# Registers used as loaded, and a 32-deep ring of message tiles, in a graph network kernel

## The chip, the cores and the metric

The kernel runs on one core of a Trainium2 chip. The metric is the device time in microseconds of one execution; a measurement is a median over executions. The core has five engines that matter here: TensorE (PE, with its weight loads shown as PEld), VectorE (DVE), ScalarE (ACT), GpSimd (POOL) and SyncE (SP). Each runs its own instruction stream in order. A name with a q (DVEq, ACTq, SPq) is that engine's sequencer: register work, loads of registers and the issuing of DMAs.

## What is computed

The reference is two graph layers over 12,500 nodes of 128 features and 212,500 edges, each followed by a residual sum and a layer norm.

```python
# layer 0: message passing, summed at the source node of each edge
h = silu(edge_attr @ W1 + b1); weights = h @ W2 + b2
messages = node_feats[dst] * weights
aggregated = segment_sum(messages, src, N)
x = layernorm(x + concat([x @ Wself + bself, aggregated]) @ Wcat + bcat)
# layer 1: means of neighbours in both directions, then a GRU cell
a_in, a_out = seg_mean(feat_in[src], dst, N), seg_mean(feat_out[dst], src, N)
x = layernorm(x + gru_cell(concat([a_in, a_out]), x))
```

## The kernel before

The kernel goes through stages in order of time. It prepares weights and tables (0 to 650 us); it computes the edge messages and scatters them, sorted by source, into the DRAM tensor `msgs` (to 2516 us); it sums them by node, the first aggregation (to 3252 us); it updates the nodes (to 3506 us); it gathers and sums neighbour rows for both directions, the second aggregation (to 8020 us); and it runs the GRU.

**The first aggregation.** The sorted edges are cut into units of 256 edges, each of which falls in one block of 128 nodes. There are V0 = 928 units, in 29 iterations (IT0) of NS = 32. Where a unit begins (row 0 of `vtab` in DRAM) and where its block stands in the accumulator (`blk0` in SBUF) are data, so they are read into registers, 32 at a time, once per iteration. For each unit:

- SP (even units, line 431) or ACT (odd units, line 707) issues one DMA that loads 256 rows of `msgs` into a slot of `mtile`; they do so in `row_loads`, which begins each iteration with `load_table`: one load of 32 registers and one copy (`snap`) for each of them (lines 320 and 321). Each load waits in `need(..., s["sum0_ready"], it * NS + k - S0 + 1)` until TensorE has summed the unit that held the slot before.
- GpSimd (`keys0`, line 581) turns the node numbers of four units (a quad) into numbers within the block, `local`, once the quad has landed.
- VectorE (`onehot0`, line 1120) makes a one-hot matrix of each unit in `oh0`. It does this one quad ahead of its sums.
- TensorE (`sums0`, line 1498) multiplies one-hot and messages, two products of 128 x 128 x 128, into one of eight PSUM banks.
- VectorE (line 1138) adds the bank to the block's place in `acc_a`.

VectorE's stream in `sums0` is: load 32 registers from `blk0` (line 1124), copy them (line 1125), and then 32 times one one-hot of the next quad and one addition of this one. `mtile` and `oh0` both have S0 = 16 slots.

**The second aggregation** runs 55 iterations (IT1) of 32 units of 128 edges for each of two directions. SP loads 32 registers and issues 32 small DMAs of edge data into `edge2` (line 470); GpSimd issues 32 indirect gathers of node rows (line 605); VectorE makes one-hots (line 1245); TensorE sums (line 1542); VectorE adds (line 1256), at offsets from its own 32 registers, again read by `load_table`.

Of the kernel before, what the change touches and what calls it, by code (L numbers as in the profile page):

```python
# [4 lines left out]

N, E, D, A = 12500, 212500, 128, 8
P = 128
# [4 lines left out]
EP = NG * GE  # L13
T = NG * TG
NB = -(-N // P)
# [7 lines left out]
U0, U1 = 2 * P, P  # L23
NS = 32
V0 = -(-(E // U0 + NB) // NS) * NS
V1 = -(-(E // U1 + NB) // NS) * NS
CW = D + 1
# [48 lines left out]
def gnn_kernel(nc, x, src, dst, edge_attr, W1, b1, W2, b2, Wself, bself, Wcat, bcat,  # L76
# [15 lines left out]
    vtab = dram("vtab", [6, V1], i32)  # L92

    ctx = ExitStack()
    with ctx:
# [16 lines left out]
        blk0 = sb("blk0", [P, V0], i32)  # L112
# [5 lines left out]
        iota_row = sb("iota_row", [P, P])  # L118
# [40 lines left out]
        cut = cutter(arena, ARENA)  # L159
# [31 lines left out]
        cut = cutter(arena, ARENA)  # L191
# [7 lines left out]
        cut = cutter(src_key, T)  # L199
# [5 lines left out]
        cut = cutter(arena, ARENA)  # L205
# [5 lines left out]
        cut = cutter(acc_a, NBP * CW)  # L211
# [6 lines left out]
        cut = cutter(acc_b, NBP * CW)  # L218
# [12 lines left out]
        cut = cutter(arena, ARENA)  # L231
# [12 lines left out]
        cut = cutter(acc_a, NBP * CW)  # L244
# [25 lines left out]
        bank = [ctx.enter_context(nc.psum_tensor(f"bank{i}", [P, 512], f32)) for i in range(8)]  # L270
# [11 lines left out]
        s = {n: sem(n) for n in names}  # L282
# [22 lines left out]
        def by_digit(eng, hot, digit, c, op):  # L305
# [6 lines left out]
                at += HC * n  # L312
            return last

        def registers(eng, name, n):
            return [eng.alloc_register(f"{name}{i}") for i in range(n)]

        def load_table(eng, regs, row, v, top):

            eng.load(regs, vtab[row:row + 1, bass.ds(v, len(regs))])  # L320
            return [eng.snap(r, min_val=0, max_val=top) for r in regs]

        @block.sync
        def _(sp):
# [98 lines left out]
            regs0 = registers(sp, "sp_row", NS)  # L424
# [31 lines left out]
            sp.wait_ge(s["aux_in"], 16 * 9)  # L456

            regs1 = registers(sp, "sp_edge", NS)
            sp.wait_ge(s["dst_sorted"], 1)  # L460
            for half, row in ((0, 2), (1, 4)):
                first = half * V1 // TG

                def edge2_loads(it):
                    offs = load_table(sp, regs1, row, it * NS, EP - U1)
                    for q in range(4):
                        need(sp, s["sum1_ready"], first + it * 4 + q - 3)
                        for k in range(TG):
                            of = msgs[bass.ds(offs[q * TG + k], U1), D:D + 2] if half == 0 else dlist[bass.ds(offs[q * TG + k], U1), :]
                            sp.dma_start(edge2[:, q * TG + k, :], of).then_inc(edge2_in[q], 16)  # L470

                edge2_loads(0)
                with sp.Fori(1, IT1) as it:
                    edge2_loads(it)
# [145 lines left out]
        def _(act):  # L620
# [73 lines left out]
            edge_group(NG // 2 - 1, after=0)  # L694

            regs0 = registers(act, "act_row", NS)
            act.wait_ge(s["tables_out"], 48)
            for b in range(2):
                act.wait_ge(scattered[b], 16 * TG * (NG // 2))  # L700
            act.wait_ge(s["msg_ready"], 2 * NG)

            def row_loads(it):
                offs = load_table(act, regs0, 0, it * NS, EP - U0)
                for k in range(1, NS, 2):
                    need(act, s["sum0_ready"], it * NS + k - S0 + 1)
                    act.dma_start(mtile[:, k % S0, :, :], msgs[bass.ds(offs[k], U0), :].rearrange("(p i) c -> p i c", i=2)).then_inc(mtile_in[k % S0 // 4], 16)

            row_loads(0)
            with act.Fori(1, IT0) as it:  # L710
# [51 lines left out]
        def _(dve):  # L762
# [354 lines left out]
            regs = registers(dve, "dve_blk", NS)  # L1117

            def onehot0(q, k):
                v.tensor_tensor(oh0[:, (4 * q + k) % S0], iota_row[:, :].rearrange("p (o n) -> p o n", o=1).to_broadcast([P, 2, P]),  # L1120
                                local[:, q % 2, k, :].rearrange("p (i o) -> p i o", o=1).to_broadcast([P, 2, P]), ALU.is_equal).then_inc(s["oh0_ready"], 1)

            def sums0(it, last=False):
                dve.load(regs, blk0[0:1, bass.ds(it * NS, NS)])  # L1124
                at = [dve.snap(r, min_val=0, max_val=NB * D) for r in regs]
                for q in range(NS // 4):
                    more = not (last and q == NS // 4 - 1)
                    if more:
                        dve.wait_ge(s["local_ready"], it * (NS // 4) + q + 2)
                    for k in range(4):  # L1130
                        if more:
                            onehot0(q + 1, k)

# [4 lines left out]
                        v.tensor_tensor(a, a, bank[n % 8][:, 0:D], ALU.add).then_inc(s["add0_done"], 1)  # L1138

            dve.wait_ge(s["local_ready"], 1)  # L1140
            for k in range(4):
# [92 lines left out]
            for half, (row, blk, acc) in enumerate(((3, blk1s, acc_b), (5, blk1d, acc_a))):  # L1234
                v0 = half * V1

                def sums1(it):
                    at = load_table(dve, regs, row, it * NS, NB * CW)
                    first = half * V1 // TG + it * 4

                    def onehots1(q):
                        dve.wait_ge(edge2_in[q], 16 * TG * (it + half * IT1 + 1))
                        need(dve, s["sum1_ready"], first + q - 1)
                        for k in range(TG):
                            last = v.tensor_scalar(oh1[:, q % 2, k, :], iota_row[:, :], blk[:, bass.ds(it * NS + q * TG + k, 1)], edge2[:, q * TG + k, 0:1], ALU.add, ALU.is_equal)  # L1245
                        last.then_inc(s["oh1_ready"], 1)

                    onehots1(0)
                    for q in range(4):
                        if q < 3:  # L1250
                            onehots1(q + 1)
                        dve.wait_ge(s["sum1_ready"], first + q + 1)
                        for k in range(TG):
                            need(dve, s["add1_done"], v0 + it * NS + q * TG + k)
                            a = acc[:, bass.ds(at[q * TG + k], CW)]
                            v.tensor_tensor(a, a, bank[q % 2 * 4 + k // 2][:, (k % 2) * 256:(k % 2) * 256 + CW], ALU.add).then_inc(s["add1_done"], 1)  # L1256

                sums1(0)
                with dve.Fori(1, IT1) as it:
                    sums1(it)  # L1260

                dve.wait_ge(s["add1_done"], (half + 1) * V1)
                sums = acc[:, 0:NB * CW].rearrange("p (n c) -> p n c", c=CW)
                any_row = 1 - half
                us.mark(v.tensor_scalar(aux9[:, :, :, any_row], sums[:, :, D:CW].to_broadcast([P, NB, 3]), 1.0, None, ALU.min))
                us.link(v.tensor_scalar(rcnt[:, :, :], sums[:, :, D:CW], 1.0, None, ALU.max))
                us.link(v.reciprocal(rcnt[:, :, :], rcnt[:, :, :]))
                for part in (slice(0, 2 * SB), slice(2 * SB, NB)):
                    n = part.stop - part.start  # L1270
                    v.tensor_tensor(sums[:, part, 0:D], sums[:, part, 0:D], rcnt[:, part, :].to_broadcast([P, n, D]), ALU.mult).then_inc(s["g_mean"], 1)
# [39 lines left out]
        def _(pe):  # L1311
# [181 lines left out]
            def sums0(it):  # L1493
                for k in range(NS):
                    pe.wait_ge(s["oh0_ready"], it * NS + k + 1)
                    need(pe, s["add0_done"], it * NS + k - 7)
                    for i in range(2):
                        last = mm(bank[k % 8][:, 0:D], oh0[:, k % S0, i, :], mtile[:, k % S0, i, 0:D], start=(i == 0), stop=(i == 1))  # L1498
                    last.then_inc(s["sum0_ready"], 1)

            pe.wait_ge(s["msg_ready"], 2 * NG)
# [96 lines left out]
```

## Time and profile before

| | us |
|---|---|
| median of 3 runs (lowest, highest) | 8351.24 (8341.68, 8357.66) |
| the profiled execution, its own time | 8366.66 |
| its span, first to last instruction | 8365.0 |
| the first aggregation, 2516 to 3252 | 736 |
| the second aggregation, 3506 to 8020 | 4514 |

The profile is one execution, with the start and duration of each instruction. "Busy" is the time an engine worked; "idle before" is the time it stood still just ahead of an instruction, with what ended the wait. "Issue" as what ended it means that nothing the profile shows was waited for: the engine's own sequencer was at register work. PEclk is the TensorE clock granted, 1.0 for 2.4 GHz and 0.5 for 1.2 GHz. Matmul records are pipelined, so TensorE shown busy need not be at its peak. The DMA share is the mean busy share of 16 DMA engines.

### The profile page before, as it was taken

The numbers are of one execution on the slowest core, as the hardware profiler recorded it, in microseconds if no ns is written. First come the engines' busy times: TensorE is split into PE (matmuls) and PEld (weight loads), VectorE is DVE, ScalarE is ACT, GpSimd is POOL, SyncE is SP. The second block draws the span as 40 slices with busy tenths as digits, with TensorE's granted clock in tenths as the row PEclk, the third lists the DMA queues.
The fourth block names the chain that finished last, engine by engine and source line by source line (L and its number), as shares of the span: only waits on it lengthen the run. The fifth ranks groups of instructions, "written<-read, shape, count | busy, mean of one in ns | idle before, by whom it ended". The sixth has DMA issues, their size and how long they took to land.

```text
span 8365.0 us, 131491 instructions
## 1 busy us (share of the span) xinstructions
PE 4763.1 (57%) x27076; PEld 4075.6 (49%) x27076; DVE 4424.6 (53%) x16824; ACT 837.7 (10%) x1997; POOL 5233.1 (63%) x5536
## 2 busy tenths in 40 slices
PE   2899999999987778633333333332333333333368
PEld 2677777777776777533333333332333333333334
DVE  7666666666666665444444444444444444444445
ACT  0223222222220000100000000000000000000023
POOL 4477777777771000277777777776777777777710
PEclk8778778777787886566666666665666666666579
DMA  2233333333335564222222222225222222222332
GB/s 63 82 110 113 108 109 112 107 108 111 108 104 173 175 181 128 69 53 53 53 53 53 53 53 53 53 53 45 53 53 53 53 53 53 53 53 53 51 58 76
DMA packets 954826, 668.11 MB, mean 80 GB/s; under 512 B 643688, under 2 KB 839389, under 8 KB 954128
## 3 DMA queue, kind: packets, MB, share of 16 engines
q0 software_dynamic: 170112, 360.70, 16.3%
q1 hardware_dynamic: 717719, 241.33, 12.7%
q10 hardware_dynamic: 66944, 65.50, 2.6%
q8 instruction: 20, 0.33, 0.0%
q14 instruction: 31, 0.25, 0.0%
HBM read 515.84 MB, written 138.14 MB: 78 GB/s over the span
## 4 chain that ended last, share of the span: by engine, by line
POOL 39%; issue 14%; PE 11%; DMA 2%; ACTq 1%; DVEq 1%; DVE 1%; SPq 1%; POOLq 0%; ACT 0%
POOL arena L605 39%; PE bank L1498 4%; DMA arena<-msgs 1%; PE bank L1568 1%; ACTq L320 1%; PE bank L1527 1%; PE bank L1569 1%; PE bank L1570 1%; DVEq L1124 1%; PE bank L1517 1%; SPq L470 1%; DMA arena<-x1d,arena 1%; PE bank L1525 1%; PE bank L1526 0%; PE bank L1560 0%
## 5 line engine op out<-in xcount | busy, mean ns | idle before, releaser
L605 POOL DMA_INDIRECT arena<-x1d,arena x3520 | 3377.8, 960 | 1130.5 <-issue 1072.6
L1542 PE MATMUL bank<-arena 128*128 128x129 f32 x7040 | 1497.8, 398 | 3031.6 <-DMA arena<-x1d,arena 1522.0
L1542 PEld LDWEIGHTS bank<-arena 128*128 128x128 f32 x7040 | 1392.8, 303 | 3136.6 <-issue 3100.5
L570 POOL DMA_INDIRECT msgs<-arena x1664 | 1659.4, 997 | 660.8 <-issue 512.7
L1256 DVE TENSOR_TENSOR acc_b<-acc_b,bank 128x129 f32 x1760 | 510.7, 290 | 900.8 <-PE bank L1542 697.8
L1256 DVE TENSOR_TENSOR acc_a<-acc_a,bank 128x129 f32 x1760 | 510.6, 290 | 889.9 <-PE bank L1542 687.2
L1245 DVE TENSOR_SCALAR arena<-iota_row,blk1d,arena 128x128 f32<-128x128 f32 x1760 | 473.6, 365 | 370.8 <-issue 368.0
L1498 PE MATMUL bank<-arena 128*128 128x128 f32 x3712 | 552.2, 319 | 202.4 <-DVE arena L1120 202.2
L1245 DVE TENSOR_SCALAR arena<-iota_row,blk1s,arena 128x128 f32<-128x128 f32 x1760 | 467.8, 360 | 373.4 <-issue 373.4
L1498 PEld LDWEIGHTS bank<-arena 128*128 128x128 f32 x3712 | 534.5, 223 | 220.1 <-issue 215.3
L1470 PE MATMUL bank<-arena 128*128 (+1 forms) x3328 | 620.6, 344 | 0.2 <-DVE arena L1056 0.2
L1438 PE MATMUL bank<-arena,w1pad 64*128 64x128 f32 x3328 | 614.4, 338 | 0.4 <-ACT arena L660 0.4
L1446 PE MATMUL bank<-w2s,acc_b 128*128 128x128 f32 x3328 | 586.2, 330 | 0.0
L1470 PEld LDWEIGHTS bank<-arena 128*128 128x128 f32 x3328 | 525.2, 240 | 65.6 <-issue 32.7
L1446 PEld LDWEIGHTS bank<-w2s,acc_b 128*128 128x128 f32 x3328 | 497.7, 229 | 120.6 <-issue 120.6
L1438 PEld LDWEIGHTS bank<-arena,w1pad 64*128 64x128 f32 x3328 | 519.9, 235 | 56.1 <-issue 26.3
L1120 DVE TENSOR_TENSOR arena<-iota_row,arena 128x256 f32<-128x256 f32 x928 | 394.4, 425 | 223.2 <-POOL arena L581 134.1
L743 ACT ACTIVATE arena<-bank 128x384 f32<-128x384 f32 x98 | 47.7, 486 | 4551.7 <-PE bank L1561 4550.8
L581 POOL TENSOR_TENSOR arena<-arena,src_key 128x8 f32<-128x8 f32 x232 | 69.3, 299 | 659.8 <-DVE arena L1120 327.9
L1070 DVE CUSTOM_DVE_ANT_0 arena<-bank,earlier 128x128 bf16<-128x128 f32 x1664 | 381.8, 286 | 84.3 <-PE bank L1402 84.2
L1062 DVE TENSOR_TENSOR arena<-bank,arena 128x512 f32<-128x512 f32 x416 | 286.4, 689 | 224.8 <-PE bank L1446 223.5
L666 ACT ACTIVATE acc_b<-bank,b1c 128x512 f32<-128x512 f32 x416 | 285.9, 687 | 891.4 <-PE bank L1438 891.4
(256 smaller groups left out, 4538.5 us busy)
## 6 DMA issues: line engine op xcount, KB each, us to landing
arena<-rows SPq DMA_DIRECT2D x208, 512.0 KB
arena<-msgs SPq DMA_DIRECT2D x464, 136.0 KB, 2.6
arena<-msgs ACTq DMA_DIRECT2D x464, 136.0 KB, 3.0
arena<-x1d,arena POOLq DMA_INDIRECT x3520, 2.5
arena<-msgs SPq DMA_DIRECT2D x1760, 1.0 KB
arena<-dlist SPq DMA_DIRECT2D x1760, 1.0 KB
msgs<-arena POOLq DMA_INDIRECT x1664
arena<-xwin SPq DMA_DIRECT2D x208, 64.0 KB
```

The source lines that it names most:

```text
L570: pool.indirect_dma_start(msgs, bass.IndirectOffsetOnAxis(ap=pos[:, b, j:j + 1], axis=0), mrow[:, b, j, :], None).then_inc(scattered[b], 16)
L605: pool.indirect_dma_start(grow[:, sl, 0:D], None, x1d, bass.IndirectOffsetOnAxis(ap=edge2[:, sl, 1:2].bitcast(i32), axis=0)).then_inc(gath ...
L1062: v.tensor_tensor(mrow[:, b, 4 * h:4 * h + 4, 0:D], bank[2 + h][:, :].rearrange("p (j d) -> p j d", j=4), xjs[:, h, :].rearrange("p (j d) ...
L1070: last = v.tensor_tensor_reduce(out=junk[:, j, :], in0=bank[6][:, k * P:(k + 1) * P], in1=earlier[:, :], scale=1.0, scalar=0.0, op0=ALU.mu ...
L1120: v.tensor_tensor(oh0[:, (4 * q + k) % S0], iota_row[:, :].rearrange("p (o n) -> p o n", o=1).to_broadcast([P, 2, P]), local[:, q % 2, k, ...
L1245: last = v.tensor_scalar(oh1[:, q % 2, k, :], iota_row[:, :], blk[:, bass.ds(it * NS + q * TG + k, 1)], edge2[:, q * TG + k, 0:1], ALU.add ...
L1256: v.tensor_tensor(a, a, bank[q % 2 * 4 + k // 2][:, (k % 2) * 256:(k % 2) * 256 + CW], ALU.add).then_inc(s["add1_done"], 1)
L1438: last = mm(bank[h][:, k * P:(k + 1) * P], w1pad[:, 4 * h + k, :], attr_t[0:TG * A, :], start=True, stop=True)
L1446: last = mm(bank[2 + h][:, k * P:(k + 1) * P], ht[:, b, h, k * P:(k + 1) * P], w2s[:, :], start=False, stop=(k == 3))
L1470: last = mm(bank[4 + h][:, k * P:(k + 1) * P], wsel[:, b, j, :], win[:, b, bass.ds(wide * j, 1), :].rearrange("p o d -> p (o d)"), start=T ...
L1498: last = mm(bank[k % 8][:, 0:D], oh0[:, k % S0, i, :], mtile[:, k % S0, i, 0:D], start=(i == 0), stop=(i == 1))
L1542: last = mm(bank[q % 2 * 4 + k // 2][:, (k % 2) * 256:(k % 2) * 256 + CW], oh1[:, q % 2, k, :], grow[:, q * TG + k, :], start=True, stop=True)
```

## The change

Two things are changed. First, `load_table` allocates new registers for each use, loads them, and wraps them with `donate=True`, so that the offsets are the loaded registers themselves and not copies; after the loop body they are freed. It is used in all four places: SP and ACT in the first aggregation, SP in the second, VectorE in both. VectorE's own load in `sums0` now goes through it too. Second, `mtile` gets S0 = NS = 32 slots, with eight landing semaphores in place of four, and `oh0` a ring of its own of SO = 8.

```diff
-        S0 = 16
+        S0, SO = NS, 8
         mtile = cut(S0 * 2 * RW).rearrange("p (s i c) -> p s i c", s=S0, i=2)
-        oh0 = cut(S0 * 2 * P).rearrange("p (s i n) -> p s i n", s=S0, i=2)
+        oh0 = cut(SO * 2 * P).rearrange("p (s i n) -> p s i n", s=SO, i=2)
...
-        def load_table(eng, regs, row, v, top):
-            eng.load(regs, vtab[row:row + 1, bass.ds(v, len(regs))])
-            return [eng.snap(r, min_val=0, max_val=top) for r in regs]
+        def load_table(eng, name, n, of, top):
+            regs = registers(eng, f"{name}{next(serial)}_", n)
+            eng.load(regs, of)
+            return regs, [eng.snap(r, donate=True, min_val=0, max_val=top) for r in regs]
+
+        def release(eng, regs):
+            for r in regs:
+                eng.free_register(r)
...
             def row_loads(it):
-                offs = load_table(sp, regs0, 0, it * NS, EP - U0)
+                regs, offs = load_table(sp, "sp_row", NS, vtab[0:1, bass.ds(it * NS, NS)], EP - U0)
                 for k in range(0, NS, 2):
                     need(sp, s["sum0_ready"], it * NS + k - S0 + 1)
                     sp.dma_start(mtile[:, k % S0, :, :], ...).then_inc(mtile_in[k % S0 // 4], 16)
+                release(sp, regs)
...
             def sums0(it, last=False):
-                dve.load(regs, blk0[0:1, bass.ds(it * NS, NS)])
-                at = [dve.snap(r, min_val=0, max_val=NB * D) for r in regs]
+                regs, at = load_table(dve, "dve_blk", NS, blk0[0:1, bass.ds(it * NS, NS)], NB * D)
```

The same edit stands in ACT's `row_loads`, in SP's `edge2_loads` and in VectorE's `sums1`; the one-hot slots are indexed modulo SO in place of S0.

## Rows read from the trace of the kernel before

**Rows 1.** The page: the span, and the chain that ended last.

```profile
span 8365.0 us, 131491 instructions
POOL 39%; issue 14%; PE 11%; DMA 2%; ACTq 1%; DVEq 1%; DVE 1%; SPq 1%; POOLq 0%; ACT 0%
```

**Rows 2.** Windows by stage; columns in the first row.

```profile
core 0: us, PE busy (x) PEld busy (x) DVE busy (x) ACT busy (x) POOL busy (x), PEclk, DMA share, GB/s
2516.00:3252.00 736.00, 552.21 (x3712) 534.51 (x3712) 506.42 (x1856) 0.00 (x0) 70.12 (x233) 0.82 0.59 176
...
3506.00:5700.00 2194.00, 731.15 (x3440) 680.45 (x3440) 963.09 (x3450) 0.00 (x0) 1661.79 (x1738) 0.61 0.27 53
```

**Rows 3.** Waits of 3506 to 8020: engine, line, released by: us, times, longest.

```profile
POOL arena L605 <- issue: 1072.6, 3514, 1.9
POOL arena L605 <- DMA arena<-msgs: 36.8, 2, 19.9
POOL arena L605 <- DMA arena<-dlist: 21.1, 4, 14.5
```

**Rows 4.** Groups of 2516 to 3252: busy us, mean ns | idle before, releasers.

```profile
L1120 DVE TENSOR_TENSOR arena<-iota_row,arena 128x256 f32<-128x256 f32 x928 | 394.4, 425 | 223.2 <-POOL arena L581 134.1 <-issue 89.1
L1138 DVE TENSOR_TENSOR acc_a<-acc_a,bank 128x128 f32 x928 | 266.8, 287 | 8.6 <-PE bank L1498 7.0 <-DVE acc_a L1138 0.4 <-issue 0.2
```

**Rows 5.** Timeline of the first aggregation: start us, us, instruction, [idle before].

```profile
2526.98 1.43 DVE L1120 TENSOR_TENSOR arena<-iota_row,arena 128x256 f32<-128x256 f32 x4 [13.44 <-POOL arena L581]
...
2897.17 0.43 DVE L1120 TENSOR_TENSOR arena<-iota_row,arena 128x256 f32<-128x256 f32 x1
...
2897.70 0.43 DVE L1120 TENSOR_TENSOR arena<-iota_row,arena 128x256 f32<-128x256 f32 x1
...
2902.27 0.43 DVE L1120 TENSOR_TENSOR arena<-iota_row,arena 128x256 f32<-128x256 f32 x1 [3.95 <-POOL arena L581]
...
2907.74 0.42 DVE L1120 TENSOR_TENSOR arena<-iota_row,arena 128x256 f32<-128x256 f32 x1 [3.24 <-issue]
...
2912.20 0.29 DVE L1138 TENSOR_TENSOR acc_a<-acc_a,bank 128x128 f32 x1 [0.23 <-PE bank L1498]
...
2913.05 0.29 DVE L1138 TENSOR_TENSOR acc_a<-acc_a,bank 128x128 f32 x1 [0.23 <-PE bank L1498]
```

**Rows 6.** The chain that ended last, 2890 to 2908: start us, us, what.

```profile
2890.97 0.34 ACTq L707
...
2891.71 1.22 ACTq L320
...
2893.11 3.58 ACTq L320
...
2897.87 0.34 ACTq L707
...
2898.45 3.29 DMA arena<-msgs
...
2904.70 2.10 DVEq L1124
```

**Rows 7.** Instructions of lines 321, 1124 and 1125, 2516 to 3252: ns min/median/max, starts.

```profile
L321 SPq MOVE  x464: 29/29/38, 2521.9 to 3224.9; - x155
...
L1124 DVEq TENSOR_LOAD <-blk x29: 2098/2110/2158, 2527.1 to 3231.2; - x29
...
L1125 DVEq FUSED_REGOPS  x116: 60/223/239, 2529.3 to 3234.1; - x116
```

**Rows 8.** Issues of one burst on SP's queue.

```profile
2897.49 4.48 SPq L431 DMA_DIRECT2D arena<-msgs  x8
```

**Rows 9.** Short windows of the first aggregation; columns as in Rows 2.

```profile
2889.00:2892.00 3.00, 3.00 (x30) 3.00 (x29) 3.00 (x13) 0.00 (x0) 0.20 (x1) 1.00 0.92 262
2900.00:2902.00 2.00, 0.00 (x0) 0.00 (x0) 0.00 (x0) 0.00 (x0) 0.00 (x0) 1.00 0.89 255
2904.00:2906.00 2.00, 1.96 (x9) 1.67 (x8) 0.50 (x2) 0.00 (x0) 0.33 (x1) 0.50 1.07 377
```

More of the change, by code:

```diff
@@ L4 @@
 from contextlib import ExitStack
+from itertools import count
 N, E, D, A = 12500, 212500, 128, 8
@@ L313, in by_digit @@
             return last
+        serial = count()
         def registers(eng, name, n):
             return [eng.alloc_register(f"{name}{i}") for i in range(n)]
-        def load_table(eng, regs, row, v, top):
-            eng.load(regs, vtab[row:row + 1, bass.ds(v, len(regs))])
-            return [eng.snap(r, min_val=0, max_val=top) for r in regs]
+        def load_table(eng, name, n, of, top):
[5 more added lines that the diff above has]
+                eng.free_register(r)
         @block.sync
@@ L456, in _ @@
             sp.wait_ge(s["aux_in"], 16 * 9)
-            regs1 = registers(sp, "sp_edge", NS)
             sp.wait_ge(s["dst_sorted"], 1)
@@ L464, in edge2_loads @@
                 def edge2_loads(it):
-                    offs = load_table(sp, regs1, row, it * NS, EP - U1)
+                    regs, offs = load_table(sp, "sp_edge", NS, vtab[row:row + 1, bass.ds(it * NS, NS)], EP - U1)
                     for q in range(4):
@@ L470, in edge2_loads @@
                             sp.dma_start(edge2[:, q * TG + k, :], of).then_inc(edge2_in[q], 16)
+                    release(sp, regs)
                 edge2_loads(0)
@@ L694, in _ @@
             edge_group(NG // 2 - 1, after=0)
-            regs0 = registers(act, "act_row", NS)
             act.wait_ge(s["tables_out"], 48)
@@ L703, in row_loads @@
             def row_loads(it):
-                offs = load_table(act, regs0, 0, it * NS, EP - U0)
+                regs, offs = load_table(act, "act_row", NS, vtab[0:1, bass.ds(it * NS, NS)], EP - U0)
                 for k in range(1, NS, 2):
@@ L707, in row_loads @@
                     act.dma_start(mtile[:, k % S0, :, :], msgs[bass.ds(offs[k], U0), :].rearrange("(p i) c -> p i c", i=2)).then_inc(mtile_in[k % S0 // 4], 16)
+                release(act, regs)
             row_loads(0)
@@ L1116, in _ @@
             us.link(v.memset(acc_a[:, :], 0.0))
-            regs = registers(dve, "dve_blk", NS)
             def onehot0(q, k):
-                v.tensor_tensor(oh0[:, (4 * q + k) % S0], iota_row[:, :].rearrange("p (o n) -> p o n", o=1).to_broadcast([P, 2, P]),
+                v.tensor_tensor(oh0[:, (4 * q + k) % SO], iota_row[:, :].rearrange("p (o n) -> p o n", o=1).to_broadcast([P, 2, P]),
                                 local[:, q % 2, k, :].rearrange("p (i o) -> p i o", o=1).to_broadcast([P, 2, P]), ALU.is_equal).then_inc(s["oh0_ready"], 1)
             def sums0(it, last=False):
-                dve.load(regs, blk0[0:1, bass.ds(it * NS, NS)])
-                at = [dve.snap(r, min_val=0, max_val=NB * D) for r in regs]
+                regs, at = load_table(dve, "dve_blk", NS, blk0[0:1, bass.ds(it * NS, NS)], NB * D)
                 for q in range(NS // 4):
@@ L1138, in sums0 @@
                         v.tensor_tensor(a, a, bank[n % 8][:, 0:D], ALU.add).then_inc(s["add0_done"], 1)
+                release(dve, regs)
             dve.wait_ge(s["local_ready"], 1)
@@ L1237, in sums1 @@
                 def sums1(it):
-                    at = load_table(dve, regs, row, it * NS, NB * CW)
+                    regs, at = load_table(dve, "dve_sum", NS, vtab[row:row + 1, bass.ds(it * NS, NS)], NB * CW)
                     first = half * V1 // TG + it * 4
@@ L1256, in sums1 @@
                             v.tensor_tensor(a, a, bank[q % 2 * 4 + k // 2][:, (k % 2) * 256:(k % 2) * 256 + CW], ALU.add).then_inc(s["add1_done"], 1)
+                    release(dve, regs)
                 sums1(0)
@@ L1497, in sums0 @@
                     for i in range(2):
-                        last = mm(bank[k % 8][:, 0:D], oh0[:, k % S0, i, :], mtile[:, k % S0, i, 0:D], start=(i == 0), stop=(i == 1))
+                        last = mm(bank[k % 8][:, 0:D], oh0[:, k % SO, i, :], mtile[:, k % S0, i, 0:D], start=(i == 0), stop=(i == 1))
                     last.then_inc(s["sum0_ready"], 1)
```

1 line of the change is left out of this document (removed).

## The prediction

> **What bounds the kernel now.** I read the page first. The chain that ended last is mostly GpSimd with its gathers [rows 1], which is the second aggregation. Its waits show that GpSimd stood still 1072.6 us for its own sequencer, between gathers, and only 36.8 + 21.1 = 57.9 us for SP's edge loads, in six waits of 3520 gathers [rows 3]. So that stage, 4514 us, goes at GpSimd's pace, with DMA at 0.27 of its time and VectorE at 963 of 2194 us [rows 2]. Faster register work on SP or VectorE finds nothing to shorten there, apart from its first iteration.
>
> The first aggregation, 736 us, is another matter. Nobody is busy all of it: VectorE works 506, DMA 0.59 of the time [rows 2]. The groups by line say who waits: VectorE's one-hots stand 134.1 us for GpSimd's keys and 89.1 us for "issue"; its additions wait for TensorE 7.0 us in all [rows 4]. The timeline shows where in an iteration both stops lie. One-hots follow each other at 0.53 us (2897.17, 2897.70), then nothing for 3.95 us until keys come (2902.27), four more units, and nothing for 3.24 us, the register load and copies (2907.74) [rows 5]. VectorE's 29 register loads start from 2527.1 to 3231.2, so the mean period is 704.1 / 28 = 25.15 us for 32 units [rows 7]. Of that, 32 x 0.533 = 17.1 is work.
>
> The chain tells what the 3.95 us are [rows 6]. ACT issues the last load of an iteration, then loads the table's address (1.22) and the table (3.58), copies, issues (0.34), the data take 3.29 more, and only then do GpSimd, VectorE and TensorE go on. That last load had waited for a slot, so it was issued when 16 units were left in the ring. From 2890.97, its issue, to 2898.45 + 3.29 = 2901.74, when the next quad has landed, 10.8 us pass; VectorE is a quad ahead, so what it has left is 12 units x 0.533 = 6.4 us. The difference, 4.4 us, is the stop seen, give or take the slot's own delay.
>
> **The copies.** VectorE's table is read from SBUF in 2.11 us, and 116 fused copies, four per iteration, follow at a median of 0.223 us [rows 7]. In the shown iteration the load ends at 2906.80 and the one-hot starts at 2907.74 [rows 5, 6]: 0.94 us, of which the copies with their gaps are about 0.89 (three of 0.223, a short one of 0.08, and the gaps). They are on the path, because VectorE alone sets the pace. 28 boundaries x 0.89 = 24.9 us. The load itself stays, also under its new name. On SP and ACT 16 copies an iteration live (464 / 29 [rows 7]) and cost about 0.9 us each time: ACT's table load ends at 2896.69 and its first issue starts at 2897.87, 1.18 us, of which some 0.3 is each issue's own register work [rows 6]. With the deeper ring they lie beside work and are worth nothing, but once: ahead of the very first load, 0.9 us. If that cover were gone they would be worth 28 x 0.9 = 25 us more, but those are already within the stop that I remove. In the second aggregation the copies on SP stand ahead of its first issue, which I count at 0.8 us, a little less than VectorE's 0.89 for the same work; in the other 109 iterations, GpSimd's 32 gathers hide them. The six waits for SP there could each move by some us either way; I count nothing, and keep 57.9 us as the most they could give.
>
> **The ring.** With 32 slots, the last load of an iteration waits only for the last unit of the iteration before. SP's and ACT's way from one iteration's last issue to the next one's first is 2897.87 - 2891.31 = 6.6 us now and 5.7 without copies [rows 6], and it then begins with a whole iteration in the ring. Some 3 of the 5.7 us are VectorE's own boundary, so some five units come free meanwhile; each queue issues its two or three late ones (4.48 - 0.34) / 7 = 0.59 us apart [rows 6, 8], against 1.07 us in which two units are used, and is level again after about five loads. The first unit of the next iteration is thus issued some 2.5 us after its slot is free, and lands by about 7 us after, with the 3.3 us of landing [rows 6] and one for queueing. It is wanted 28 units, 15 us, into the iteration. So the lead is about 8 us where it is -4.4 now. What is late next is VectorE's boundary, and nothing in between.
>
> VectorE waited for keys 134.1 us in all [rows 4]; 13.44 of it is the start of the stage [rows 5], which the ring cannot help, and I leave some 2 us for the quad behind that one. 119 us go. Below, the stop could survive in part: the bound is 0 to 119. I take 119 because the lead of 8 us is nearly twice the stop.
>
> The eight slots of `oh0` cost nothing: one-hot n + 4 is made after the addition of n - 1, which already waited for TensorE's product of n - 1, and that frees the slot of n - 4. Eight semaphores in place of four change no count of instructions on GpSimd, and it is busy 70 of 736 us [rows 2].
>
> **Does DMA keep up?** One unit is 128 partitions x 1088 B = 139 KB, an iteration 4.46 MB. The period after is 25.15 - 119 / 28 - 0.89 = 20.0 us, that is 223 GB/s and, from 0.59 now, a share of 0.74. In full stretches DMA moved 255 to 377 GB/s, 262 of them with TensorE and VectorE both busy [rows 9]. At 262, 4.46 MB take 17.0 us. It fits, with 15% to spare.
>
> **TensorE's clock.** It is granted 0.82 on average in this stage [rows 2]. At 1.2 GHz a unit takes TensorE 2913.05 - 2912.20 = 0.85 us, and VectorE then waits for it [rows 5]; at 2.4 GHz it keeps up. In the whole stage this costs 7.0 us [rows 4], since four units of lead absorb a short slow stretch. With one stop an iteration in place of two I expect less: 0 to 7.0 us off, I take 4.
>
> **Sum.** 119 + 24.9 + 0.9 + 0.8 + 4 = 149.6, say 150 us. The profiled execution took 8366.66, so it would take 8217. It stands 15.4 over the median of the three runs; from the median, 8351.24 - 150 = 8201 us, 1.8% less. Across the boundary two one-hots would start 3.24 - 0.89 + 0.62 = 2.97 us apart (0.62 from the last one-hot's start to its addition's end). The floor of the period, 31 x 0.533 + 2.97, is 19.5 us, 28 x 5.65 = 158 us off: 8191.
>
> **Rivals.**
>
> *A slow clock at each boundary.* TensorE still stands 2.97 - 0.43 = about 2.5 us at VectorE's boundary (0.43 is a unit at 2.4 GHz, half of the 0.85). For it: the row at 2904 shows 0.5 after the stop at 2898 to 2902 [rows 9]. Against: that stop was longer, and most waits on TensorE are short. Were each boundary followed by 10 us at 1.2 GHz, TensorE would do 12 units where VectorE wants 19, 3.7 us behind, less 1.1 of lead: a period of 22.6 and 28 x 2.55 = 71 us saved: 8280. The Trainium skill, page TensorE: Matmul & The Clock Gate, section HAM oscillation, says that the array falls to the half clock when waits part the bursts of matmuls, and pays for the return each time. By it the time would lie toward this rival; the granted 0.82 agrees in kind.
>
> *The same, and slower than before.* If the clock never recovered, 31 x 0.853 + 2.97 = 29.4 us a period, 4.25 x 28 = 119 us more: 8470. It decides against the change once the slow share of the stage passes some 60% (the period passes 25.15 when the mean unit takes 0.715 us); it is 36% now, with two stops. Nothing in the profile points there but the many falls.
>
> *DMA becomes the bound.* If twice as deep a queue of random rows moved only 208 GB/s, the period would be 21.4 us, 105 us saved: 8246. For: the landings spread over 3.3 us even now. Against: 262 GB/s beside both engines [rows 9].
>
> *The copies stay*, because the compiler makes them again or splits the loads: the 24.9 and 1.7 us are lost, 8228.
>
> **How the numbers follow.** The forecast, 8201, has 0.70; its own range is 8185 to 8222. The slow clock in some measure has 0.09, DMA 0.07, the copies staying 0.07, slower than before 0.03, and 0.04 is for something unseen, half of it around no change. The range for 8 in 10 is 8183 to 8245: below, the floor with 8 us for the scatter of runs; above, the copies and DMA cases. This kernel's three runs span 0.19%, so 0.2% is what can be told from no change. Faster 0.94, same 0.02, slower 0.04.
>
> **What would show it.** In the profile after: VectorE's one-hots waiting for GpSimd's keys some 15 us in this stage in place of 134; "issue" ahead of them 2.35 us, 28 times, 66 us in place of 89; line 1125 without copies; 29 loads of VectorE's registers 20 us apart; the stage 590 us long at a DMA share of 0.73; the second aggregation within 10 us of 4514. The prediction is wrong if keys are still waited for at each iteration, if TensorE's products are waited for by more than 20 us, or if the second aggregation moves.

## The result, and the profile after

The changed kernel takes 8204.91 us (median of 4 runs, 8195.06 to 8212.00) against 8351.78 for the kernel before: a ratio of 0.9825, 95% interval 0.9808 to 0.9842. The forecast was 8201, range 8183 to 8245. The profiled execution is the longest of the four, 8212.0 us with a span of 8210.4, so the two traces differ by 154.6 us.

The groups by line of the first aggregation answer to [rows 4] (busy us, mean ns | idle before, releasers):

```profile
L1505 PE MATMUL bank<-arena 128*128 128x128 f32 x3712 | 507.4, 302 | 92.9 <-DVE arena L1126 92.6
...
L1126 DVE TENSOR_TENSOR arena<-iota_row,arena 128x256 f32<-128x256 f32 x928 | 388.6, 419 | 81.2 <-issue 67.1 <-POOL arena L589 14.1
L1143 DVE TENSOR_TENSOR acc_a<-acc_a,bank 128x128 f32 x928 | 260.5, 281 | 3.3 <-PE bank L1505 1.5 <-issue 0.4 <-DVE acc_a L1143 0.4
```

Three releasers matter here. The wait for GpSimd's keys fell from 134.1 to 14.1 us. What is left are two waits at the start of the stage, 12.6 and 1.5 us. "Issue" fell from 89.1 to 67.1: the register load without its copies. The wait of the additions for TensorE fell from 7.0 to 1.5. Together 147.5 us.

VectorE's register loads answer to [rows 7] (ns min/median/max, first and last start):

```profile
L324 DVEq TENSOR_LOAD <-blk x29: 2098/2102/2149, 2531.9 to 3086.7; - x29
```

From the first to the last it is 554.8 us for 28 periods, 19.81 us each, against 704.1 and 25.15. That is 149.3 of the 154.6 us. The rest nets to 5.3 us: up to the first of these loads this trace is 4.8 us longer, the gathers of the second aggregation span 4484.3 us in place of 4490.4, 6.1 less, and the stretches ahead of them and behind them are 1.9 and 2.1 us shorter. Differences of that size come between any two traces here, as the experiments show, and nothing can be read from them.

The windows answer to [rows 2] for the two stages, and then show one boundary between iterations (columns as in [rows 2]):

```profile
2521.00:3106.00 585.00, 507.41 (x3712) 493.02 (x3712) 502.29 (x1856) 0.00 (x0) 88.73 (x233) 0.92 0.73 221
3362.00:5560.00 2198.00, 767.96 (x3456) 714.22 (x3456) 968.39 (x3452) 0.00 (x0) 1664.93 (x1744) 0.60 0.27 53
2706.00:2711.00 5.00, 5.00 (x40) 4.83 (x38) 5.00 (x20) 0.00 (x0) 0.83 (x2) 1.00 0.98 293
2711.00:2714.00 3.00, 0.77 (x7) 0.56 (x5) 0.58 (x3) 0.00 (x0) 0.20 (x1) 1.00 0.24 74
2714.00:2719.00 5.00, 4.90 (x27) 4.88 (x28) 4.92 (x19) 0.00 (x0) 0.84 (x2) 0.66 0.56 148
```

The stage is 585 us long at a DMA share of 0.73, and TensorE is granted 0.92 of its clock where it was 0.82. It still stands at the boundary (0.77 us busy of 3), and the clock still falls behind it (0.66 in the next 5 us), but not for long: in the windows 2719 to 2724 and 2724 to 2729 it is 1.00 again. With TensorE and VectorE both busy throughout, DMA moved 293 GB/s at 2706.

In the timeline the boundary is the only stop left in an iteration; compare [rows 5]:

```profile
2710.51 0.42 DVE L1126 TENSOR_TENSOR arena<-iota_row,arena 128x256 f32<-128x256 f32 x1
2710.85 0.28 DVE L1143 TENSOR_TENSOR acc_a<-acc_a,bank 128x128 f32 x1
...
2713.54 0.43 DVE L1126 TENSOR_TENSOR arena<-iota_row,arena 128x256 f32<-128x256 f32 x1 [2.42 <-issue]
...
2714.10 2.27 PE L1505 MATMUL bank<-arena 128*128 128x128 f32 x13 [2.33 <-DVE arena L1126]
```

And ACT's table is gone from the chain that ended last, where [rows 6] had it (start us, us, what). It runs along TensorE and VectorE, and through VectorE's register load:

```profile
2699.90 10.81 PE bank L1505 x87
...
2711.32 2.10 DVEq L324
...
2713.54 0.44 DVE arena L1126
...
2714.10 7.98 PE bank L1505 x53
```

### The profile page after: what moved, and what is told of

It reads as the page before. It is cut to its first block, busy times and chain, and to the rows that moved or that the text cites. A ratio compares the mean times of both kernels' runs of the same rounds, so it can differ in the third digit from the quotient of the medians.

```text
span 8210.4 us, 129812 instructions
## 1 busy us (share of the span) xinstructions
PE 4776.0 (58%) x27076; PEld 4086.6 (50%) x27076; DVE 4414.9 (54%) x16824; ACT 838.0 (10%) x1997; POOL 5251.1 (64%) x5536
## 4 chain that ended last, share of the span: by engine, by line
POOL 38%; issue 14%; PE 13%; DMA 1%; DVEq 1%; SPq 1%; DVE 1%; POOLq 0%; ACT 0%; ACTq 0%
POOL arena L613 38%; PE bank L1505 6%; PE bank L1575 1%; DVEq L324 1%; PE bank L1534 1%; PE bank L1576 1%; PE bank L1577 1%; SPq L477 1%; DMA arena<-x1d,arena 1%; PE bank L1524 1%; PE bank L1549 1%; PE bank L1532 1%; PE bank L1533 1%; PE bank L1567 0%; PE bank L1574 0%
## 5 line engine op out<-in xcount | busy, mean ns | idle before, releaser
L1549 PE MATMUL bank<-arena 128*128 128x129 f32 x7040 | 1559.6, 410 | 2963.2 <-DVE arena L1251 1704.3
L1505 PE MATMUL bank<-arena 128*128 128x128 f32 x3712 | 507.4, 302 | 92.9 <-DVE arena L1126 92.6
L1126 DVE TENSOR_TENSOR arena<-iota_row,arena 128x256 f32<-128x256 f32 x928 | 388.6, 419 | 81.2 <-issue 67.1
L589 POOL TENSOR_TENSOR arena<-arena,src_key 128x8 f32<-128x8 f32 x232 | 87.8, 378 | 490.6 <-DVE arena L1126 475.6
```

Of the source, the lines that this page charges most:

```text
L1126: v.tensor_tensor(oh0[:, (4 * q + k) % SO], iota_row[:, :].rearrange("p (o n) -> p o n", o=1).to_broadcast([P, 2, P]), local[:, q % 2, k, ...
L1505: last = mm(bank[k % 8][:, 0:D], oh0[:, k % SO, i, :], mtile[:, k % S0, i, 0:D], start=(i == 0), stop=(i == 1))
L1549: last = mm(bank[q % 2 * 4 + k // 2][:, (k % 2) * 256:(k % 2) * 256 + CW], oh1[:, q % 2, k, :], grow[:, q * TG + k, :], start=True, stop=True)
```

## The experiments

Eleven kernels ran, in three jobs, each on a chip of its own. By their speed these are of two kinds. On one chip the kernel before took 8370 us, near the first result; this is called the first kind. On the two others it took 10301 us, the second kind. So a time is only ever compared with a time of the same job or, by their 10301, between those two jobs, and the periods of the first aggregation, read from the traces, across all. That this may be done shows in a trace of the kernel before on the second kind of chip (one run, 10309.4 us): VectorE's loads from 3253.2 to 3958.6, a period of 25.19 us against 25.15.

| kernel | median us | kernel before, same job | ratio, 95% interval | period, first aggregation |
|---|---|---|---|---|
| changed again | 8223.6 | 8370.2 | 0.9825, 0.9811 to 0.9839 | 19.83 |
| copies back | 10171.0 | 10300.9 | 0.9876, 0.9860 to 0.9893 | 20.50 |
| ring of 16 | 10177.9 | 10300.9 | 0.9882, 0.9865 to 0.9898 | 22.64 |
| address loaded twice | 10096.0 | 10300.9 | 0.9805, 0.9789 to 0.9821 | 19.78 |
| address loaded three times | 10099.4 | 10300.9 | 0.9807, 0.9790 to 0.9823 | 19.80 |
| two tables | 10143.2 | 10301.4 | 0.9835, 0.9821 to 0.9850 | 20.97 |
| three tables | 8405.9 | 8370.2 | 1.0039, 1.0024 to 1.0054 | 25.97 |
| one-hots over the load | 8218.6 | 8370.2 | 0.9812, 0.9796 to 0.9828 | 19.69 |
| copies back, second only | 8226.2 | 8370.2 | 0.9820, 0.9801 to 0.9839 | 19.80 |
| second aggregation alone | 10251.9 | 10301.4 | 0.9943, 0.9931 to 0.9955 | 25.17 |

A period is the last start less the first start of VectorE's 29 register loads, over 28. The changed kernel itself ran on the first kind alone. On the second kind the two kernels with repeated address loads stand in for it: they keep its period, and what they add is hidden, as shown below.

**Copies back.**

```diff
-            return regs, [eng.snap(r, donate=True, min_val=0, max_val=top) for r in regs]
+            return regs, [eng.snap(r, min_val=0, max_val=top) for r in regs]
```

> The changed kernel with one thing undone: the offsets are copies of the loaded registers again; the ring stays 32 deep. Theory: the copies cost only where they lie on VectorE's path at the boundary between iterations of the first aggregation, 28 x 0.89 = 25 us, and about 1.7 us at two starts: 8205 + 27 = 8232 us. VectorE's 'issue' idle ahead of the one-hots is 91 us in place of 67.1, the period 20.7 us in place of 19.8; the second aggregation does not move. Rival 1: the copies on SP and ACT count too, since each of their queues has little slack: then the period grows by more than 1 us and keys are waited for. Rival 2: copies cost nothing and the ring did it all: 8205 us.

The period is 20.50 us, 0.69 more than the changed kernel's, 19 us over 28. VectorE's waits (us, times, longest):

```profile
DVE arena L1126 <- issue: 90.1, 28, 3.3
DVE arena L1126 <- POOL arena L589: 12.3, 2, 10.5
```

"Issue" is back at 90.1 and keys are waited for twice only, 12.3 us, as in the changed kernel: the copies on SP and ACT are free with a ring of 32, those on VectorE cost 0.7 to 0.8 us an iteration and not 0.89. The time, though, is 72 to 75 us over that of the kernels with repeated address loads in the same job, which have the changed kernel's period. 19 of it are the periods. Most of the rest lies in the second aggregation, below.

**Ring of 16.**

```diff
-        S0, SO = NS, 8
+        S0, SO = 16, 8
```

> The changed kernel with the message ring back at 16 slots (one-hot ring of 8 kept, no copies). Theory: the stop at the next table comes back, shorter than before by the 0.9 us of ACT's copies: 4.3 - 0.9 = 3.4 us x 28 = 95 us, so 8205 + 95 = 8300 us, with 110 us of waits for GpSimd's keys in the first aggregation where there are 14.1, and a TensorE clock there of about 0.8 where it is 0.92. Rival 1: without the copies the 16 slots would have been enough, 8205 us. Rival 2: the stop returns in full, 119 us: 8324 us; the copies of ACT were then not in the chain.

```profile
DVE arena L1126 <- POOL arena L589: 131.8, 51, 7.8
DVE arena L1126 <- issue: 17.0, 7, 2.4
```

The period is 22.64 us, 2.83 more than with 32 slots, 79 us over 28. The copies alone, with the ring of 16, took the period from 25.15 to 22.64: 2.51 us, where with the ring of 32 they were worth 0.69. So the two parts don't add: the ring alone is worth 4.65 us a period (25.15 to 20.50), the copies alone 2.51, both 5.34. In time it is 79 to 82 us over the kernels with repeated address loads, and TensorE's granted clock in the stage is 0.87 (0.92 with 32 slots).

Where the 2.51 us lie is read from the idle time ahead of the first one-hots of two quads in each iteration. They stand like this in one iteration of this trace:

```profile
3582.11 0.43 DVE L1126 TENSOR_TENSOR arena<-iota_row,arena 128x256 f32<-128x256 f32 x1 [2.29 <-POOL arena L589]
3586.76 0.42 DVE L1126 TENSOR_TENSOR arena<-iota_row,arena 128x256 f32<-128x256 f32 x1 [2.42 <-POOL arena L589]
```

In [rows 5] the same two were 3.95 and 3.24. On the mean of the 28 boundaries the stop for keys is 4.21 us before and 2.60 here, and the stop at VectorE's register load is 3.22 before and 2.40 here. So the copies give 0.82 us at VectorE's boundary and 1.61 at the stop for keys, 2.43 of the 2.51. The load is not hidden: the second stop, 2.42 us above, is as long as the changed kernel's, where only the load stands there. GpSimd is named for it in most iterations (51 waits, and "issue" only 7 times) because the keys of that quad came late too, inside the load. Of the 1.61, 1.00 is on ACT's queue, whose way from one iteration's last issue to the next one's first is 6.03 us in place of 7.03: ACT's copies. Another 0.4 is that the keys follow the quad's last issue after 3.3 us in place of 3.7, and why they do is open. The forecast of 3.4 us for the stop had taken off the 0.9 of ACT's copies alone.

**Repeated table loads.** Two kernels called the load again with the same registers and the same address:

```diff
-            eng.load(regs, of)
+            for _ in range(times):
+                eng.load(regs, of)
```

It stands in SP's and ACT's loads of the first aggregation alone, with times=2 and times=3.

> The changed kernel, but SP and ACT each load the 32 registers of the first aggregation twice per iteration (the second load fetches the same values). It adds about 1.2 + 3.6 = 4.9 us to each queue per iteration. Theory: the ring of 32 leaves a lead of 7 to 8 us, and a queue needs 16 x 0.57 + 6.0 + 4.9 = 20.0 us per iteration against a period of 19.8: nothing to speak of is lost, 0 to 10 us, 8205 to 8215 us. Rival: the time of the table loads is still in the chain in part (the gain came only from removing the copies and some of the load): then up to 28 x 4.9 = 137 us come back, 8342 us.

> As the kernel with two table loads per iteration, but with three. Theory: what limits a deep ring is no longer its lead but the queue's own time, 16 x 0.57 + 6.0 + 2 x 4.9 = 24.9 us per iteration against 19.8: the period becomes 24.9 us, 28 x 5.1 = 143 us lost, 8348 us, and keys are waited for again. Rival: only the lead counts, 7 us against 9.8 added: 2.8 x 28 = 78 us lost, 8283 us.

Both kept the changed kernel's period, 19.78 and 19.80. But the trace shows that they did not do what was meant. Of the kernel with three, lines of its register loads:

```profile
L325 SPq TENSOR_LOAD <-vtab_ptr x84: 831/848/2545, 3252.2 to 3783.6; - x84
...
L325 SPq TENSOR_LOAD <-vtab x29: 3508/3596/3773, 3239.6 to 3784.5; - x29
```

The table was loaded 29 times, once an iteration; only the load of its address was repeated. So they show no more than that 1 or 2 us added to SP and ACT are hidden. Two more kernels loaded the table into register sets of their own and used a part of each. The edit with three, on SP, and the same on ACT; the kernel with two uses one half of each:

```diff
                 regs, offs = load_table(sp, "sp_row", NS, vtab[0:1, bass.ds(it * NS, NS)], EP - U0)
+                regs3, offs3 = load_table(sp, "sp_rowc", NS, vtab[0:1, bass.ds(it * NS, NS)], EP - U0)
+                regs2, offs2 = load_table(sp, "sp_rowb", NS, vtab[0:1, bass.ds(it * NS, NS)], EP - U0)
+                offs = offs[:8] + offs3[8:16] + offs2[16:]
```

> The changed kernel with three loads of 32 registers in SP's and ACT's streams per iteration of the first aggregation, each into registers of its own that are used (the earlier runs with repeated loads kept a single table load, and repeated only the address load). It adds 2 x (1 + 3.6) = 9.2 us to each queue per iteration. Theory: the limit is the queue's own time, 16 x 0.57 + 6.0 + 9.2 = 24.3 us against a period of 19.8: 28 x 4.5 = 126 us more than the changed kernel. Rival 1: only the lead of 7 us counts: 2.2 x 28 = 62 us more. Rival 2: the time of table loads still stands in the chain in full: 28 x 9.2 = 258 us more.

> The changed kernel with two loads of 32 registers per iteration in SP's and ACT's streams, each used for half of the units. With three, the period was 25.97 us and the queues never waited. Theory: it is the queue's own time that bounds, and a table with its address costs it 4.7 us, so the period is 26.0 - 4.7 = 21.3 us against 19.8, 28 x 1.5 = 42 us more than the changed kernel. Rival: the lead of 7 us covers the one added load of 4.7 us, and nothing is lost.

With three the period is 25.97 us, 0.8 longer than before the change, and the kernel is 182 us slower than the changed one beside it (126 were expected). With two it is 20.97 (21.3 expected), 1.16 x 28 = 32 us. The chain through SP in the kernel with three tables (start us, us, what; pieces under 0.3 us left out) is without a gap:

```profile
2895.46 0.33 SPq L441
2896.27 2.33 SPq L324
2898.80 3.54 SPq L324
2902.36 1.02 SPq L324
2903.49 3.57 SPq L324
2907.09 1.00 SPq L324
2908.19 3.59 SPq L324
2912.05 0.34 SPq L441
2912.65 0.33 SPq L441
```

From 2896.27 to 2912.05 are 15.8 us of tables, then 16 issues at about 0.6: 26 us, the period. In the changed kernel, SP's queue waited for slots (us, times, longest):

```profile
SPq L438 <- PE bank L1505: 133.7, 305, 1.1
```

That is 4.8 us an iteration of slack. In the kernels with two and three tables that row is missing altogether: in this stage SP never waits for a slot.

An added table with its address is 4.6 us (1.0 + 3.6 in the rows above), which alone would fit into 4.8. But without the waits the first address load of an iteration is longer as well: 2.33 us in the rows above, and a median of 2.20 in the kernel with two tables, where it is 1.18 in the changed kernel. So one added table lengthens SP's way from one iteration's last issue to the next one's first by 5.8 us (6.0 to 11.9 in the medians), which is 1.0 over the slack; the period grew by 1.16. Two lengthen it by 10.7 us (to 16.8), 5.9 over the slack; the period grew by 6.16. What is longer than SP's slack lengthens the period one for one. So with 32 slots the limit is not how early a unit lands but how much work SP and ACT have per iteration: had only the lead of 7 to 8 us counted, 5.8 us would have been covered. My sum had looked only at the lead.

**One-hots over the load.** The last quad's four additions go first, then the next quad's four one-hots, then the load:

```diff
                     more = not (last and q == NS // 4 - 1)
-                    if more:
+                    ahead = more and q < NS // 4 - 1
+                    if ahead:
...
-                        if more:
+                        if ahead:
...
+                    if more and not ahead:
+                        dve.wait_ge(s["local_ready"], it * (NS // 4) + q + 2)
+                        for k in range(4):
+                            onehot0(q + 1, k)
```

> The changed kernel with one thing moved: in the last quad of an iteration of the first aggregation VectorE makes its four additions first and then the next quad's four one-hots, so that these run while its sequencer loads the 32 registers. Theory: the four additions, each waiting for the one before, take 0.42 us each in place of lying between one-hots (cost 1.7 us), and 1.9 of the 2.4 us of idle time are covered: 0.5 us less per iteration, 15 us less than the changed kernel. 'Issue' ahead of the one-hots nearly vanishes and idle time ahead of the first addition of an iteration, 0.5 to 0.8 us, takes its place. Rival: VectorE's sequencer runs at most one instruction ahead of the engine, so nothing is covered, and the additions in a row cost 1 us per iteration: 28 us more.

The period is 19.69 us, 0.14 less than the changed kernel's in the same job, 4 us over 28; 8218.6 against 8223.6 us, which the intervals do not part.

```profile
L1126 DVE TENSOR_TENSOR arena<-iota_row,arena 128x256 f32<-128x256 f32 x928 | 378.9, 416 | 50.5 <-POOL arena L589 50.5
L1144 DVE TENSOR_TENSOR acc_a<-acc_a,bank 128x128 f32 x928 | 258.9, 279 | 23.6 <-PE bank L1510 11.6 <-DVE acc_a L1144 11.6 <-issue 0.4
```

The idle time ahead of the one-hots fell from 81 to 50.5 us, so the load is covered in part, and the rival with a cost of 28 us is out: on the mean 1.08 of the load's 2.10 us lie over VectorE's own work, 0.01 in the changed kernel. But additions in a row wait for each other and for TensorE, 23.2 us in place of 1.9, which takes most of the gain; 15 us were expected and 4 came. It is the fastest kernel by its period and by no clear margin in time.

**Which chip, and the second aggregation.** The changed kernel was run again, then with the copies back in the second aggregation alone:

```diff
-                regs, offs = load_table(sp, "sp_edge", NS, vtab[row:row + 1, bass.ds(it * NS, NS)], EP - U1)
+                regs, offs = load_table(sp, "sp_edge", NS, vtab[row:row + 1, bass.ds(it * NS, NS)], EP - U1, donate=False)
...
-                    regs, at = load_table(dve, "dve_sum", NS, vtab[row:row + 1, bass.ds(it * NS, NS)], NB * CW)
+                    regs, at = load_table(dve, "dve_sum", NS, vtab[row:row + 1, bass.ds(it * NS, NS)], NB * CW, donate=False)
```

Last, the kernel before with that part of the change alone. In its edit against the changed kernel, the two lines above stay as they were, and the first aggregation goes back:

```diff
-        S0, SO = NS, 8
+        S0, SO = 16, 16
...
-                regs, offs = load_table(sp, "sp_row", NS, vtab[0:1, bass.ds(it * NS, NS)], EP - U0)
+                regs, offs = load_table(sp, "sp_row", NS, vtab[0:1, bass.ds(it * NS, NS)], EP - U0, donate=False)
```

The same donate=False stands in ACT's load there and in VectorE's. Its period, 25.17 us, is that of the kernel before.

> The changed kernel itself, beside the others, as their point of comparison, since the last four ran on a chip on which the kernel before took 10301 us and not 8352. Theory: on a chip like the first, 147 us less than before. On a chip like the second, 28 x 5.35 = 150 us less in the first aggregation, as on the first, and some 50 us less in the second aggregation, where SP's instructions come late there, 205 us in all. Rival: the gain is the same 150 us on both, and the two runs with repeated address loads were faster for another reason.

> The changed kernel, with the copies back in the second aggregation alone (SP's and VectorE's tables there). Theory: on a chip like the first they lie beside GpSimd's gathers and cost 1 us at the start. On a chip like the second, where SP's instruction stream sets the pace of that stage, they cost 0.5 us in each of 110 iterations, 55 us. Rival: no difference on either chip.

> The kernel before with one part of the change alone: no copies in the second aggregation (SP's and VectorE's tables there); in the first aggregation both the copies and the ring of 16 are as before. Theory: GpSimd's gathers set the pace, so 1 us less than the kernel before and no more, on a chip like the first. On a chip like the one on which the kernel before took 10301 us, SP's instruction stream sets the pace of that stage and it is 50 us less. Rival: some of the 147 us came from the second aggregation on any chip; then this is 10 us or more faster than before.

> The kernel before, for a trace of it on the chip of this job. On a chip like the first: period of the first aggregation 25.15 us, second aggregation 4514 us. On a chip like the second: the same period, and the edge stage and the second aggregation some hundred us longer each, with gaps between SP's instructions that wait for nothing.

On the first kind of chip the changed kernel is again 146.6 us faster (147 expected), and the copies of the second aggregation cost nothing that can be told: 8226.2 against 8223.6 us, and the gathers span 4490.2 against 4492.2. On the second kind, the part alone is worth 49.5 us (50 expected; 0.9943, 0.9931 to 0.9955). The 205 us expected of the whole change there have no run of their own; the kernels with repeated address loads, which carry the whole change, are 205 and 201 us faster. The gathers' first and last starts, of the kernel before and of the one with that part alone, both there:

```profile
L605 POOL DMA_INDIRECT arena<-x1d,arena x3520: 947/955/10963, 4235.9 to 9922.9; - x196
```

```profile
L613 POOL DMA_INDIRECT arena<-x1d,arena x3520: 948/955/10959, 4236.2 to 9876.1; - x196
```

They span 5687.0 and 5639.9 us, 47 us apart. With copies back everywhere the span is 5685.4. In the four other kernels without copies in this stage it is 5645.6 and 5632.1 (repeated address loads), 5649.1 (ring of 16) and 5654.0 (two tables). So the copies go with 31 to 55 us in this stage, whatever the first aggregation does. Why they count there is in the waits. SP's in the second aggregation, of the kernel before on the first kind of chip:

```profile
SPq L470 <- PE bank L1542: 1879.1, 327, 13.7
```

and of the same kernel on the second kind, SP's and then GpSimd's, the latter to be held against [rows 3]:

```profile
SPq L470 <- remote: 45.2, 3, 22.7
SPq L470 <- PE bank L1542: 11.0, 1, 11.0
...
POOL arena L605 <- DMA arena<-dlist: 664.0, 104, 19.9
POOL arena L605 <- DMA arena<-msgs: 631.0, 91, 11.2
```

On the first kind SP waited 1879 us for free slots, and GpSimd hardly ever for SP's loads. On the second kind SP waited 56 us and GpSimd 1295 us for SP's loads. The same program, with the same DMA sizes, is there bound by the rate at which SP gets through its instructions, so fewer of them is time saved. That it is SP's copies that count, and not VectorE's, was not isolated: both were taken out together. The chain that ended last makes it likely: over this stage SP's copies (line 321) are 2.9% of it, and VectorE's are under 0.3%.

The issues themselves last no longer: the median is 0.33 us in both traces, and in a full burst they start 0.52 us apart in both. What differs is that register instructions of the same line now and then take 0.7 us or a multiple of it, and that gaps of 0.7 us stand between them with nothing waited for. Line 470 from 5000 to 6000 in the trace on the first kind, then in that on the second (ns min/median/max), then five late pieces of the chain on the second (start us, us, what):

```profile
L470 SPq FUSED_REGOPS  x765: 37/46/51, 5000.0 to 5999.9; - x192
```

```profile
L470 SPq FUSED_REGOPS  x636: 2/46/1378, 5000.2 to 5997.5; - x159
```

```profile
5009.27 0.70 issue
5010.01 0.68 SPq L470
5010.71 0.70 SPq L470
5011.43 0.70 issue
5012.13 0.71 SPq L470
```

Gaps of over 0.3 us ahead of SP's instructions that wait for no semaphore add up to 1973 us in this stage on the second kind, and to 1 us on the first.

## Why the prediction was right, point by point

**What bounds the kernel.** That only the first aggregation could give anything held: 149.3 of 154.6 us lie in its 28 periods. The gathers of the second span 4490.4 us before and 4484.3 in the first trace after, but 4492.2 when the changed kernel ran again, so nothing is to be read from it. On the first kind of chip the experiments bear it out from both sides. On the second kind the statement would have been wrong, by some 50 us: "Faster register work on SP or VectorE finds nothing to shorten there" rests on GpSimd setting the pace, and there it does not.

**The copies.** On the path, as said, but the term was 24.9 us and measured 22.0 by the idle time, 19 by the periods with the copies back. I had put down the whole stretch of 0.94 us between load and one-hot but 0.05; 0.12 us of it stays in the chain after (2713.42 to 2713.54). The 0.9 and 0.8 us for the copies at two starts are too small for these traces to show.

**SP's and ACT's copies.** Free behind a deep ring, as said: with the copies back, keys were waited for 12.3 us in all. That they were already within the stop of the shallow ring was right too, and undersized: with 16 slots all copies together were worth 2.51 us a period: 0.82 at VectorE's boundary, 1.00 on ACT's queue, and 0.4 in how soon the keys follow the issues, for which no cause is shown.

**The ring.** 119 us were predicted off the wait for keys and 120.0 came off. Nothing of the stop survived. With the copies back and the ring of 32 the period is 20.50 us, so the ring alone takes 4.65 off it and is the larger part by either order of counting. The argument behind it was right in its result and wrong in what it took for the margin. It counted a lead of 8 us; what is really scarce is SP's and ACT's time per iteration, 4.8 us of slack on SP. The change did not test it, but one added table load, 5.8 us on SP's way, used it up, where a lead of 8 us would have covered it. A forecast for a longer register load by the lead would have failed.

**DMA.** A share of 0.74 and 223 GB/s were worked out, 0.73 and 221 measured. The rival that DMA becomes the bound is out: it moved 293 GB/s beside both engines.

**The clock.** 4 us were put down, of 0 to 7.0 possible, and 5.5 came. The rival that each boundary is followed by a long stretch at 1.2 GHz is out by its price: the clock fell after the 2.33 us stop at 2711 to 0.66 of the next 5 us, but the additions waited 1.5 us in the whole stage. Worked out from the stage's mean of 0.92, TensorE is at the lower level for some 94 of the 585 us, an estimate; the rival, with 10 us at each of 28 boundaries, had 280. The rule in the Trainium skill (TensorE: Matmul & The Clock Gate, HAM oscillation), that waits between bursts bring the clock down, agrees with the trace: 0.66 behind the stop. With one stop in an iteration in place of two the mean rose from 0.82 to 0.92. That VectorE's pace, 0.53 us a unit where TensorE needs 0.43 at the full clock, is what lets TensorE catch up is argued from these figures; no run tested it.

**The sum.** 149.6 us predicted from the median, 146.9 measured between medians, 154.6 between the two traces. The three large terms came as 120.0, 22.0 and 5.5, together 147.5 where 147.9 were put down: the sum is nearer than its terms, because the clock gave 1.5 us more and the copies gave 2.9 us less. That much is luck; the mechanism held.

## What to carry to other kernels

A stop that comes once per iteration is worth reading as a chain with a lead: how many units are left when the last slot is refilled, against how long the table load, the issue and the landing take. If the ring holds a whole iteration, such a chain stops counting, and what is left to check is whether the issuing queues have time to spare in an iteration; their own waits for slots say how much. Two parts of a change that lie in one chain don't add up: measure each with and without the other. And a count of hidden register instructions is only as hidden as the engine in front of it is slow, which one chip's trace can't vouch for on another. Added work can also cost more than its own length: once the queue no longer waited, the address load behind its last issue took 1.0 us longer.

## What the runs showed of the hardware that I had not expected

The same kernel took 8352 and 8370 us (medians) in two jobs and 10301 in two others, each within 0.4% from its lowest run to its highest. In the traces of the kernel before, the first aggregation is the same to 0.2% (25.15 and 25.19 us a period). The second aggregation's gathers span 4490 us on the one and 5687 on the other, and all ahead of the first aggregation ends at about 2516 and 3242. On the second kind SP's instructions stand apart by steps of 0.7 us though nothing is waited for, in the second aggregation and not in the first, where the issues keep their spacing. That could be instructions reaching the engine late; I did not test it, and the cause stays open. One more thing differs between the traces. With the same 131491 instructions, the one on the second kind holds 71,390 records of semaphore updates and the one on the first 179,844. The missing ones are of the stages that are longer there; in the first aggregation none is missing. So the waits by releaser are less sure in these stages on the second kind, while the starts and durations of instructions, on which the gaps of 1973 us rest, are complete. Whether what loses the records also takes the time was not tested either.

And a table load of 32 registers in the first aggregation costs SP and ACT 3.6 to 3.7 us from DRAM (medians of 3.57 to 3.74), and VectorE 2.10 to 2.11 from SBUF, on every chip and in every kernel here.
